# One queue for attention's loads in the order of their use, x in eight parts, and norm batches spread over bodies

## The reference

```python
ln_out = layernorm(hidden_states, ln1_s, ln1_b)
q, k, v = jnp.split(ln_out @ w_qkv + b_qkv, 3, axis=-1)
ctx = merge_heads(attention(split_heads(q), split_heads(k), split_heads(v), ltor_mask))
x = hidden_states + (ctx @ w_ao + b_ao)
q = layernorm(x, ln2_s, ln2_b) @ w_q + b_q
k, v = jnp.split(encoder_states @ w_kv + b_kv, 2, axis=-1)
x = x + (merge_heads(attention(..., cross_mask)) @ w_co + b_co)
return x + gelu(layernorm(x, ln3_s, ln3_b) @ w1 + b1) @ w2 + b2
```

## Time and profile before

| what | us |
|---|---|
| median of 3 runs (lowest, highest) | 1304.67 (1304.26, 1307.09) |
| the profiled execution's own time | 1298.35 |
| its span, first to last instruction | 1296.40 |
| TensorE busy | 1173.4 |
| VectorE busy | 982.0 |
| ScalarE busy | 759.7 |
| GpSimd busy | 601.7 |

### The profile page before, as it was taken

One profiled execution on the slowest core, in us unless ns is written; L12 is line 12 of the kernel. 1 busy time (PEld: TensorE's weight loads), 2 busy tenths in 40 slices (PEclk: granted clock), 3 DMA queues, 4 the chain that ended last, 5 costly groups with the idle time before them and its releaser, 6 DMA issues. The chain is left out here.

```text
span 1296.4 us, 34790 instructions
## 1 busy us (share of the span) xinstructions
PE 1173.4 (91%) x13056; PEld 988.5 (76%) x13056; DVE 982.0 (76%) x1715; ACT 759.7 (59%) x1683; POOL 601.7 (46%) x520
## 2 busy tenths in 40 slices
PE   3799999999999996899999999999999997754998
PEld 3688888888888875687787778787778785542887
DVE  3777777676666762158999889999889999894787
ACT  2577777677777764566655566655566554343332
POOL 2677777777777760133443443443443442320111
PEclk9899999999999998999999999999999998886999
DMA  9200000011111100000000000000000000000011
GB/s 364 68 3 0 0 0 0 9 36 43 32 40 32 40 18 1 1 1 1 1 1 1 2 1 1 0 0 0 0 0 0 1 1 2 1 1 0 33 40 57
DMA packets 24792, 26.98 MB, mean 21 GB/s; under 512 B 2256, under 2 KB 19984, under 8 KB 24080
## 3 DMA queue, kind: packets, MB, share of 16 engines
q1 hardware_dynamic: 23424, 24.42, 5.5%
q10 hardware_dynamic: 1296, 1.58, 0.3%
HBM read 21.79 MB, written 4.19 MB: 20 GB/s over the span
## 5 line engine op out<-in xcount | busy, mean ns | idle before, releaser
L1364 DVE TENSOR_TENSOR_SCAN late_st<-late_wT,late_st 128x512 f32<-128x512 f32 x128 | 184.3, 1440 | 4.4
L805 POOL TENSOR_TENSOR late_xm<-late_mixed,late_xa 128x512 f32<-128x512 f32 x80 | 93.6, 1178 | 156.5 <-DVE late_mixed L1336 150.2
L262 POOL TENSOR_TENSOR att_z<-att_z,att_row_max 128x512 f32<-128x512 f32 x128 | 130.7, 1042 | 11.2 <-DVE att_row_max L580 8.5
L814 POOL TENSOR_TENSOR late_st<-late_st,late_rT 128x512 f32<-128x512 f32 x32 | 40.7, 1270 | 192.3 <-DVE late_st L1364 192.3
L1358 DVE TENSOR_TENSOR late_st<-psum,late_kT 128x504 f32<-128x504 f32 x128 | 86.6, 677 | 52.4 <-PE psum L990 51.1
L875 PE MATMUL psum<-w,late_hT 128*128 128x256 f32 x512 | 121.7, 382 | 1.9 <-ACT late_hT L1120 1.9
L866 PE MATMUL psum<-late_glnT,w 128*128 128x256 f32 x512 | 117.8, 384 | 2.2 <-ACT late_glnT L1110 2.2
L875 PEld LDWEIGHTS psum<-w,late_hT 128*128 128x128 f32 x512 | 94.9, 190 | 19.9 <-issue 5.5
L866 PEld LDWEIGHTS psum<-late_glnT,w 128*128 128x128 f32 x512 | 96.3, 193 | 15.6 <-ACT late_glnT L1110 2.9
L255 POOL TENSOR_TENSOR att_z<-att_z,cross_bias 128x512 f32<-128x512 f32 x64 | 80.2, 1274 | 59.4 <-DVE att_z L573 57.8
L255 POOL TENSOR_TENSOR att_z<-att_z,self_bias 128x512 f32<-128x512 f32 x64 | 80.2, 1274 | 50.9 <-DVE att_z L573 50.9
(11 more groups left out here) (167 smaller groups left out, 2833.2 us busy)
## 6 DMA issues: line engine op xcount, KB each, us to landing
att_encT<-in_enc SPq DMA_DIRECT2D x64, 128.0 KB, 2.5
out<-x SPq DMA_DIRECT2D x16, 256.0 KB, 2.0
x<-in_x SPq DMA_DIRECT2D x1, 2048.0 KB, 11.5
w<-in_w SPq DMA_DIRECT2D x2, 1024.0 KB, 21.8
x<-in_x SPq DMA_DIRECT2D x1, 1024.0 KB, 6.9
cross_mask<-in_cross_mask SPq DMA_DIRECT2D x1, 1024.0 KB, 15.3
x<-in_x SPq DMA_DIRECT2D x1, 768.0 KB, 4.9
w_qkv<-in_w_qkv ACTq DMA_DIRECT2D x1, 768.0 KB, 15.6
```

The costliest lines, as they stand in the source:

```text
L262: nc.gpsimd.tensor_tensor(zs, zs, peak.unsqueeze(2).to_broadcast([P, PAIRS, S]), ALU.subtract).then_inc(shifted, 1)
L805: nc.gpsimd.tensor_tensor(xm[:, m % 2, :, :].rearrange("p h (b t) -> p (h b) t", t=S), mixed[:, m % 2, :, :].rearrange("p h (b t) -> p (h ...
L1364: nc.vector.tensor_tensor_scan(states, wT[:, u, half, :, :, :].rearrange("p j b t -> p (j b t)"), states, 0.0, ALU.mult, ALU.add).then_inc ...
```

## The change

The loads of ScalarE's queue move to SyncE's, which now issues: x part 0, the tables, w_qkv, x part 1, the rows and w_ao, x parts 2 to 7, and then as before. X comes in eight parts (2, 6, and six of 4 tiles). The first norm has three batches, (0, 2), (2, 8) and (8, 32); the statistics of x parts 2 to 7 are taken at the end of bodies -5 to 0, one part each. Variances come at the end of one body, and the inversion and the shift in the next, the shift now at the end of VectorE's body: batch 2 in bodies 0 and 1, the second norm's batches in 25 and 26, and in 33 and 34. Four more bodies (23 to 26) are written out instead of looped.

```diff
-X_PARTS = (2, 6, 8, 16)
+X_PARTS = (2, 6, 4, 4, 4, 4, 4, 4)
...
-    LN_PARTS = [*zip(starts, starts[1:]), (0, 24), (24, TILES)]
-    SELF_NORMS, FIRST_CROSS, ALL_NORMS = len(X_PARTS), len(X_PARTS) + 1, len(X_PARTS) + 2
+    LN_PARTS = [(0, 2), (2, 8), (8, TILES), (0, 24), (24, TILES)]
+    SELF_NORMS, FIRST_CROSS, ALL_NORMS = 3, 4, 5
...
-        NORM_AT = {2: -1, 3: 1, SELF_NORMS: TILES - 5, SELF_NORMS + 1: TILES + 1}
+        NORM_AT, STATS_AT = {2: 1, SELF_NORMS: TILES - 6, SELF_NORMS + 1: TILES + 2}, -7
...
-            with eng.Fori(0, (TILES - 8) // 4) as i:
+            with eng.Fori(0, (TILES - 12) // 4) as i:
                 for j in range(4):
                     body(0, 4 * i + (3 + j), (3 + j) % 4)
-            for n in range(TILES - 5, TILES + 3):
+            for n in range(TILES - 9, TILES + 3):
...
-            for i, loaded in enumerate(x_loaded):
+            def load_x(i):
                 cols = slice(starts[i] * C, starts[i + 1] * C)
-                sp.dma_start(core.x[:, cols], core.dram["x"][:, cols]).then_inc(loaded, 16)
+                sp.dma_start(core.x[:, cols], core.dram["x"][:, cols]).then_inc(x_loaded[i], 16)
+
+            def load_weights(phase):
+                for dst, src in core.loads[phase]:
+                    sp.dma_start(dst, src).then_inc(core.loaded[phase], 16)
+
+            load_x(0)
+            load_weights("tables")
+            load_weights("qkv")
+            load_x(1)
+            load_weights("self")
+            for i in range(2, len(X_PARTS)):
+                load_x(i)
             sp.wait_ge(zeroed, 2)
             for phase in ("cross", "gelu", "recurrent"):
-                for dst, src in core.loads[phase]:
-                    sp.dma_start(dst, src).then_inc(core.loaded[phase], 16)
+                load_weights(phase)
...
-                if i == SELF_NORMS:
-                    act.wait_ge(xn_ready, TILES)
+                if i >= SELF_NORMS:
+                    act.wait_ge(xn_ready, LN_PARTS[i][1])
...
-            for phase in ("tables", "qkv", "self"):
-                for dst, src in core.loads[phase]:
-                    act.dma_start(dst, src).then_inc(core.loaded[phase], 16)
...
             def body(k, t, u):
                 n = k * TILES + t
-                for i in range(SELF_NORMS, len(LN_PARTS)):
-                    if n_is(n, NORM_AT[i]):
-                        variances(i)
...
-                for i in range(2, len(LN_PARTS)):
-                    if n_is(n, NORM_AT[i]):
-                        shifts(i)
...
                     add_residual(*on(k, t, -1))
-                for i in range(2, SELF_NORMS):
+                for i in range(2, len(X_PARTS)):
+                    if n_is(n, STATS_AT + i):
+                        load_stats(i)
+                for i in range(2, len(LN_PARTS)):
                     if n_is(n, NORM_AT[i] - 1):
-                        load_stats(i)
                         variances(i)
+                    if n_is(n, NORM_AT[i]):
+                        shifts(i)
```

More of the change, by code:

```diff
@@ L438, in normalise @@
                 else:
-                    act.wait_ge(norm_ready, SELF_NORMS if looped(t) else [t < stop for stop in starts[1:]].index(True) + 1)
+                    act.wait_ge(norm_ready, SELF_NORMS if looped(t) else [t < stop for _, stop in LN_PARTS].index(True) + 1)
                 nc.scalar.activation(xn[:, u % 2, :], core.x[:, ds(t, C)], ACT.Identity, scale=core.rstd[:, ds(t, 1)],
```

## The result

The changed kernel takes 1281.05 us (median of 6 runs, 1278.8 to 1285.75) against 1304.26 for the kernel before in the same series (1300.67 to 1307.09): ratio 0.9827, 95% interval [0.9802, 0.9852]. That is 23.2 us less, where 16.6 were forecast; it lies under the range given. Two later series of the same kernel gave 0.9839 [0.981, 0.9869] and 0.983 [0.9811, 0.9849], so 21 to 23 us. Taken together, 77 executions of before on record have a median of 1303.89 us and the 15 of the changed kernel one of 1283.09: 20.8 us, so some 2.4 of the first series' 23.2 lie in which executions it drew. The profiled execution took 1283.38, span 1281.60: 14.8 us under the span of before. So the two spans differ by less than was forecast and the medians by more. That gap is most of what had to be explained.

What follows compares the result with a forecast made beforehand. TensorE, busy 91% of the span, was taken as the bound, so only letting it work sooner pays. Start 5.9, fill 6.3 and hand-over 4.4 sum to 16.6 us, from a median of 1304.67 to 1288.0; range 1283 to 1295.

Steps and rivals of the forecast that it cites:

- the hand-over: Self to cross attention, bodies 27, 28 and 33: norm steps moved out of TensorE's way gain 4.4 us (3 to 5.6).
- the fill: Bodies -1, 0 and 1: less norm work ahead of VectorE's masks gains 2.2, 1.1 and 3.0, sum 6.3 us (4 to 8.4).
- the start: Before TensorE's first matmul: self_mask lands earlier, VectorE waits for x part 1 until 9.0 us; gain 5.9 us (4.4 to 6.9).
- The 2.0 us: X loads: fixed cost of every DMA; paid in series, it would make the sum 15 instead of 16.6 us.
- (b): Start: small tables don't overtake, or w_qkv holds x part 1 to 15 us; no gain there, 1293.9 us; 5%.
- (e): SyncE's queue: issues stall at 4.07 us each, x part 1 lands near 28 us; 1307.2 us, slower; 4%.
- rival (a): Bodies -1 to 1: spread stats still delay TensorE each time; gain 2 us instead of 6.3, 1292.3 us; 14%.
- the 1.6 us that I charged: Body 1: stats of 4 tiles and variances of 24 take 2.3 us, 0.70 in slack, so 1.6 added to 6.87.
- Rival (d): Attention or late phases: a low-clock stretch comes at a new place, 3 to 5 us back, 1292 us; 10%.
- best case: Whole kernel: no fill stretch at 1.2 GHz, part 1 at 8; 6.9 + 8.4 + 5.6 = 20.9 us gained, 1283.8; 11%.

Runs made afterwards that it cites:

- The attention alone: Both kernels with all phases behind the attention left out and x written instead: 507.94 us before, 488.22 us changed.
- filled stops: Kernel before, with 14 unneeded identity transposes on TensorE in bodies 27 and 33 and two waits exchanged in all 64 bodies: 1310.4 us, ratio 1.0041.
- x part 1 first: Changed kernel with x part 1 issued ahead of w_qkv: 1282.05 us, ratio to before 0.9842.
- its own run: Kernel before with only the second norm's two batches moved: 1296.38 us, ratio 0.9947.
- the repeats: Both kernels run again without edit: before 1303.36 us (10 runs), changed 1283.68 (4 runs) and 1283.12 (5 runs).

## Why the prediction was wrong, point by point

The mechanisms of the sum were the right ones, with two exceptions in the fill (the clock in body -1, and body 0). What failed is the size of two terms: the hand-over, 4.4 us, where the traces show 5.6 and another 0.7 in the bodies behind it, and the fill, 6.3 us, where they show 7.3 in the first pair and 8.0 on average. With the start, which was 0.7 too high, and two small stretches, that makes 19.6 us instead of 16.6. The rest of the 23.2 is no term of the sum (see the median, below).

The lengths in us, read at the starts of the score matmuls (body n by those of tile n+2); "old" are the traces that keep this part as in before, "new" the four of the changed kernel:

| stretch | before, first trace | old: range, mean (traces) | new: mean | forecast gain | gain, first pair | gain, means |
|---|---|---|---|---|---|---|
| up to the first matmul | 19.09 | 19.0 to 19.1, 19.1 (4) | 13.9 | 5.9 | 5.3 | 5.2 |
| from there to body -2 | 7.27 | 6.9 to 7.5, 7.2 (4) | 7.4 | 0 | 0 | -0.1 |
| bodies -2 to 2, the fill | 39.75 | 39.6 to 41.3, 40.5 (7) | 32.5 | 6.3 | 7.3 | 8.0 |
| bodies 3 to 26 | 165.69 | 165.7, 165.7 (6) | 165.5 | 0 | 0.2 | 0.2 |
| bodies 27 to 34, the hand-over | 60.58 | 59.0 to 61.9, 60.7 (6) | 55.1 | 4.4 | 5.5 | 5.6 |
| bodies 35 to 60 | 183.89 | 183.9 to 184.1, 183.9 (6) | 183.3 | 0 | 0.6 | 0.7 |
| sum | | | | 16.6 | 18.9 | 19.6 |

The attention alone gave 19.7 us in the medians. (The trace with filled stops is left out, as its bodies are longer.)

- **The start, 5.9 us: measured 5.3.** The mechanism was right: the wait moves from self_mask to x part 1. It landed at 9.6 instead of 9.0. I had allowed 1.2 us in which the DMA engines are short of work; they moved 120 GB/s up to 5.60 us and 392 from there to 9.00. That this gain needed the new queue was wrong: the eight parts alone give it. Nothing in the sum hangs on it. X part 2 landed at 14.57 us, not near 12.3, and the next four 1.3 us apart each, as forecast. At 1.3 us for 512 KB no fixed cost is paid in series. The 2.0 us that the prediction takes from the Trainium skill, "DMA: Bandwidth & Descriptors", stand there in the section on DMAs issued by GpSimd ("Anatomy of one DMA"), and none here was.
- **Rivals (b) and (e)** fell: the tables land by 5.1 us; x parts 2 to 7 took 3.58 us to issue, 0.60 each, far from 3.2. VectorE did wait once for x parts 2 and 3 (1.22 us), covered as said.
- **Filling the pipe, 6.3 us: measured 7.3** in the first pair (3.5, 0.1, 3.8 against 2.2, 1.1, 3.0), 8.0 on average. Body -1: the mask comes 2.5 us earlier in its body (4.05 and 1.52 us behind the start), 2.2 forecast; the other 0.9 is the clock. The earlier trace rows has 0.82 there, 2 x 0.18 x 8.18 = 2.9 us at 1.2 GHz, and the forecast priced the low clock in body 0 alone. The last eight matmuls of the body, before and after:

```profile
37.03 2.08 PE L391 MATMUL psum<-w_qkv,att_lnT 128*128 128x128 f32 x8
```

```profile
29.21 1.16 PE L402 MATMUL psum<-w_qkv,att_lnT 128*128 128x128 f32 x8 [0.28 <-DVE att_k_heads L598]
```

Body 0 gained nothing. The stats of part 6 stand ahead of its mask (30.99 to 32.30 us), the heads come late behind it, and TensorE stops for 1.77 us, with a low clock (0.92 and 0.87) over this body and the next. That is rival (a)'s mechanism in one body; its time fell. Body 1: the 1.6 us that I charged for stats and variances cost nothing: 7.77 us at 0.87, and 6.96 at 1.00 in the run with x part 1 first. And the old body 1 was short in the trace that I read: 11.54 us there and in one other, 12.60 to 12.62 in the other five that have it.
- **The hand-over, 4.4 us: measured 5.5** in the first pair, 5.6 on average, 6.9 in the times of its own run (5.0 to 8.9). I charged the variances and cross_bias 0.3, 0.6 and 0.3 us behind the mask's slack; bodies 26, 27, 28 and 33 show 6.85 to 6.98, nothing. Without these charges the forecast has 5.6. VectorE's mask of body 26 was 0.1 us late (213.02), and the heads were ready when TensorE came to them.
- **The clock.** The forecast took its losses from one trace of before. The three pairs of whole traces lie 18.6 to 21.4 us apart at the attention's end, and 19.7 in the medians of the attention alone, as some executions pay 1.2 GHz behind bodies 1, 2 and 33 as well. Rival (d) had the sign wrong for the attention: taking stops away takes low-clock stretches away.
- **From the profiled execution to the median.** I added the same gain to a median 6.3 us above the profiled execution and said nothing of the 6.3. It was an execution with the shortest later phases of all six traces (811.5 us; the others are given with the repeats). That the spans differ by 14.8 and the medians by 21 to 23 comes from there. Of the 23.2 us of the first series, 19.7 are the attention's, some 2.4 the draw of that series (20.8 over all executions), and 1.1 are open.
- **The range, 1283 to 1295,** had 1283.8 as its best case, with all favourable bounds at once at 11%. The gain of the first pair (18.9) gives 1285.4 and the mean one (19.6) 1284.7, inside it; the draw of the first series and the open 1.1 us took the time out of it. Over all 15 executions the median is 1283.09, so by how little the range was missed or met is chance; that the sum was 3 us short is not.

What stays open: 19.7 us are the attention's, 21 to 23 are measured with all phases. The interval of the last series, [0.9811, 0.9849], is 19.7 to 24.6 us, so the difference may be none; a gain in the later phases by their new moment of beginning is neither shown nor excluded. And the kernel with filled stops leaves the cause of the falls likely and not shown.

## What to carry to other kernels

Batches of small work on an engine that is 76% busy are not free where the pipe is filling or changing phase: what stands behind their wait, and the clock afterwards, cost more than the operations; place each step one stage ahead of where its result is asked for. A small transfer that others wait for should not share the engines with a queue of big rows; cutting the big transfers did as much as ordering them. Before turning the difference of two traces into a difference of medians, take two traces of the same kernel: here they differed by 7.7 us.

## What the hardware showed that was not expected

- A 32 KB load took 11.7 us beside a queue of x with rows of 8 and 16 KB, 6.9 beside rows of 4 and 6 KB, and 1.8 on the same queue behind x part 0. The two queues went row for row (100 packets against 100 in 4 us), however long the rows.
- The same kernel's attention ended between 480.0 and 482.6 us, with the lower clock level behind different stops of the same length (body 27 takes 8.88 us in all of these traces, body 28 8.48 or 6.88). With the stops behind bodies 1, 27 and 33 removed it ended within 0.2 us in three traces and 0.8 us later in a fourth, with the later phases left out.
- Bodies 3 to 26, four of them in straight code instead of a loop: 165.63 us with the hand-over's edit alone and 165.48 to 165.51 in the changed kernel, instead of 165.69 to 165.71.
- TensorE's stop of 1.8 us in body 0 was followed by 1.2 GHz in the traces of the changed kernel and not in the one with x part 1 first.
